# A two-layer sequence model on one core: skip term, tap order and y order changed, output product behind state product and flips

## The chip, the cores and the metric
The kernel runs on one core of a Trainium2 chip. The metric is the device time of one execution in microseconds, start to end, on that core. Lower is better. The engines are called PE (TensorE), DVE (VectorE), ACT (ScalarE), POOL (GpSimd) and SP (the queue that issues the transfers).

## What is computed
Two layers over 1024 tokens of width 512 (2 sequences of 512). Attention and a binary-weight product come first, and take the first 394 us. Then comes a state-space mixer, which is nearly all of the rest, and at the end an expert layer. The mixer, cut to what matters here:

```python
dA = dt * A; cum = cumsum(dA)                       # per head, inside a chunk
scores  = (C @ B.T) * exp(cum_i - cum_j) * dt       # causal
y_intra = scores @ x
states  = (dt * exp(cum_last - cum) * B).T @ x
s       = exp(cum_last) * s + states                # carried from chunk to chunk
y_inter = (C * exp(cum)) @ s_previous
y = y_intra + y_inter + D * x                       # D * x is the skip term
g = y * silu(gate)                                  # gate = a projection of the input
g = g * rsqrt(mean(g * g) + eps) * norm_w           # mean over a group of 1024 channels
out = g @ out_w.T                                   # x, B, C = silu(conv4(projection))
```

There are 128 heads of 64 channels in 8 groups, and the state has 128 entries.

## The kernel before
The mixer handles a group of 16 heads in two halves (units) of 8 heads (512 channels). A unit has 8 steps, one for each chunk of 128 tokens, and chunks 0 to 3 are the first sequence, 4 to 7 the second. So a group has 16 steps, numbered k = 0 to 15, with chunk c = k % 8, and there are 128 steps in all. Each engine has its own in-order program for a step, written by hand, and the engines meet through semaphores. There is no scheduler: what stands first on an engine runs first, and an instruction that waits holds back all behind it.

A step "carries" (`carries(c)`) when a state comes in from the chunk before: every c but 0 and 4. It "feeds" (`feeds(c)`) when it must leave a state: every c but 3 and 7. So c = 1, 2, 5, 6 do both.

PE in a step: the transposes and product for the scores (first unit only), the gate projection for a later phase (`project_gate`, 12 matmuls), the product with the carried state (`p_inter`, L1664), one or two convolution inputs for the next unit (`conv_event`, 12 matmuls each into `p_mix`), the output product of the step before (`project_out`, 12 matmuls into `p_out`), the state product (L1677), the flips of x to token order for the next step (`flip_x`, L1582), the intra product (L1688), and a sum of squares of the step before (L1599). In c = 0 and 4 a `first_flip` (L1582 too) also flips this step's own x, which must have left the convolution. `project_out` waits for `y_split`, the low part of y of the step before.

The way of y: the intra product lands in `p_intra`. DVE adds the skip term (`xskip`, L1968) and multiplies by silu(gate) (L1973). ACT copies the high part (`high_y`, L1737), DVE subtracts to get the low part (`y_low_part`, L1921), then PE may run `project_out`. In a carrying step `xskip` is D * x plus the carried part, made by four instructions of 128 columns (L1957). In c = 0 and 4 it is D * x alone, made ahead of the taps by four instructions from and to SBUF (L1960).

The way of a convolution: ACT makes the first tap (`first_tap`, L785), DVE adds three more (`taps_of`, L807), ACT applies silu (`channels_of`, L795). For an x tile that silu also waits for the skip term of this step (`xskip_done`), since it overwrites x:

```python
if e[0] == "x":
    act.wait_ge(xskip_done, step(g, k) + 1)
```

ACT also makes the decay exponentials (L1773, four and four around `high_y`), the token copy of x (`empty_x`, L1730), which POOL turns into the operands of the state and intra products, and silu of the gate (`silu_gate`, L1783). Exponential and silu each need their own table (ACT_TABLE_LOAD). DVE also makes the arguments of the exponentials (L1912), the state's decay and sum (L2018, L2043), and reads the sum of squares of two steps ago (`mean_square`, L1930) at the head of a step. The p_inter product of step s waits for that read (`ms_read`) and for the state.

## Time and profile before
| what | value |
|---|---|
| median of 3 runs | 2118.3 us (2116.76 to 2119.54) |
| the profiled execution: its own time | 2118.76 us |
| its span, first to last instruction | 2116.9 us |
| PE busy | 1983.2 us, 94% |
| DVE busy | 1709.6 us, 81% |
| ACT busy | 1440.5 us, 68% |
| POOL busy | 1260.6 us, 60% |
| mean granted TensorE clock | 0.98 of full |

The table is read with care: a share of busy time is a mean over stages. The mixer runs from about 394 us to 2047 us of the span, a group of 16 steps takes some 205 us in the middle, and all groups but the first and the last look alike. Times inside a stretch are counted from the start of the span.

### The profile page before, as it was taken

The numbers are of one execution on the slowest core, as the hardware profiler recorded it, in microseconds if no ns is written. First come the engines' busy times: TensorE is split into PE (matmuls) and PEld (weight loads), VectorE is DVE, ScalarE is ACT, GpSimd is POOL, SyncE is SP. The second block draws the span as 40 slices with busy tenths as digits, with TensorE's granted clock in tenths as the row PEclk, the third lists the DMA queues.
The fourth block names the chain that finished last, engine by engine and source line by source line (L and its number), as shares of the span: only waits on it lengthen the run. The fifth ranks groups of instructions, "written<-read, shape, count | busy, mean of one in ns | idle before, by whom it ended". The sixth has DMA issues, their size and how long they took to land.

```text
span 2116.9 us, 34073 instructions
## 1 busy us (share of the span) xinstructions
PE 1983.2 (94%) x11288; PEld 1531.2 (72%) x11288; DVE 1709.6 (81%) x3231; ACT 1440.5 (68%) x2755; POOL 1260.6 (60%) x1185
## 2 busy tenths in 40 slices
PE   8999987799999999999999999999999999999878
PEld 4666666587877787778777777777777777777655
DVE  5677765588898889888888888888888888988976
ACT  1466633577777777777777777777778777777721
POOL 4355330256766676767676767675767666756651
PEclk9899998899999999999999999999999999999989
DMA  4000010332223322332323232222222322222201
GB/s 169 1 0 0 0 56 1 99 108 92 95 72 102 110 71 83 101 115 70 103 72 115 65 109 91 99 86 89 95 91 80 94 99 96 81 90 80 94 21 40
DMA packets 125707, 166.04 MB, mean 78 GB/s; under 512 B 37777, under 2 KB 88977, under 8 KB 121330
## 3 DMA queue, kind: packets, MB, share of 16 engines
q1 hardware_dynamic: 125554, 164.11, 24.0%
q8 instruction: 83, 1.36, 0.3%
q14 instruction: 70, 0.57, 0.1%
HBM read 159.88 MB, written 4.20 MB: 78 GB/s over the span
## 4 chain that ended last, share of the span: by engine, by line
ACT 32%; PE 26%; DVE 20%; issue 7%; POOL 0%; SPq 0%; ACTq 0%; DMA 0%; POOLq 0%; DVEq 0%
DVE conv L807 12%; ACT wq_t L1773 7%; PE p_mix L102 7%; PE p_gate_intra L102 6%; ACT L1773 5%; ACT L1783 4%; PE p_out L102 4%; DVE x_skip L1960 3%; ACT conv L785 2%; ACT x_and_gate L1783 2%; ACT yT L1737 2%; PE p_gate_intra L1688 2%; ACT y_squares L1743 2%; PE pM L102 2%; ACT w_gate L1715 1%
## 5 line engine op out<-in xcount | busy, mean ns | idle before, releaser
L2124 POOL TENSOR_TENSOR wq_t<-wq_t,cb 128x1024 f32<-128x1024 f32 x128 | 314.4, 2457 | 197.4 <-ACT wq_t L1773 159.9
L102 PE MATMUL p_out<-w_out,yT 128*128 128x512 f32 x1536 | 382.8, 399 | 24.0 <-issue 14.7
L102 PEld LDWEIGHTS p_out<-w_out,yT 128*128 128x128 f32 x1536 | 290.3, 191 | 99.8 <-issue 20.8
L102 PE MATMUL p_gate_intra<-x_high,w_gate 128*128 128x512 f32 x1024 | 350.1, 403 | 5.9 <-POOL w_gate L2107 3.4
L102 PE MATMUL p_mix<-x_high,w_x 128*128 128x512 f32 x1024 | 351.8, 405 | 2.1 <-DVE x_low L1148 1.4
L807 DVE SCALAR_TENSOR_TENSOR conv<-p_mix,unit_small,conv 128x511 f32<-128x511 f32 (+2 forms) x384 | 286.9, 747 | 63.0 <-ACT conv L785 51.4
L1773 ACT ACTIVATE wq_t<-wq_t,minus_cum 128x128 f32<-128x128 f32 x1024 | 325.3, 390 | 1.4
L795 ACT ACTIVATE x_and_gate<-conv 128x512 f32<-128x512 f32 x128 | 80.8, 632 | 253.9 <-DVE conv L807 253.7
L2165 POOL TENSOR_TENSOR x_to_state<-x_tokens,group_dt_end 128x512 f32<-128x512 f32 x96 | 120.8, 1258 | 176.6 <-ACT x_tokens L1730 176.6
L102 PEld LDWEIGHTS p_gate_intra<-x_high,w_gate 128*128 128x128 f32 x1024 | 193.4, 189 | 44.5 <-POOL w_gate L2107 3.7
L102 PEld LDWEIGHTS p_mix<-x_high,w_x 128*128 128x128 f32 x1024 | 193.7, 189 | 41.5 <-DVE conv L807 1.9
L102 PE MATMUL p_mix<-x_low,w_x 128*128 128x512 f32 x512 | 201.0, 393 | 0.0
L102 PE MATMUL p_gate_intra<-x_low,w_gate 128*128 128x512 f32 x512 | 200.9, 392 | 0.0
L1912 DVE TENSOR_TENSOR wq_t<-cum_all,tables_in 128x1024 f32<-128x1024 f32 x128 | 196.6, 1536 | 4.0 <-DMA cum_all<-cum_rows 3.0
L2170 POOL TENSOR_TENSOR x_dt<-x_tokens,tables_in 128x512 f32<-128x512 f32 x128 | 169.2, 1322 | 42.1 <-ACT x_tokens L1730 38.0
L1921 DVE TENSOR_TENSOR yT<-p_gate_intra,yT 128x512 fp32r<-128x512 f32 x128 | 88.1, 688 | 86.1 <-ACT yT L1737 86.1
L1773 ACT ACT_TABLE_LOAD x118 | 151.4, 1283 | 2.1
L826 POOL TENSOR_TENSOR w_x<-w_raw_tiles,w_x 128x512 fp32r<-128x512 f32 x64 | 83.1, 1299 | 107.3 <-DVE w_x L815 107.3
L1783 ACT ACT_TABLE_LOAD x110 | 141.1, 1283 | 1.9
L1688 PE MATMUL p_gate_intra<-wq_t,x_dt 128*64 128x128 f32 x2048 | 140.1, 279 | 0.4 <-POOL wq_t L2124 0.4
L476 DVE CUSTOM_DVE_ANT_0 pF<-pF,row_mask 128x128 f32<-128x128 f32 (+3 forms) x256 | 115.9, 526 | 24.7 <-PE pF L293 24.7
L1688 PEld LDWEIGHTS p_gate_intra<-wq_t,x_dt 128*64 128x64 f32 x2048 | 109.2, 136 | 28.2 <-issue 26.4
(242 smaller groups left out, 4435.2 us busy)
## 6 DMA issues: line engine op xcount, KB each, us to landing
cum_all<-cum_rows SPq DMA_DIRECT2D x128, 512.0 KB, 3.8
exp_cum<-exp_rows SPq DMA_DIRECT2D x192, 128.0 KB, 3.2
w_staged<-in_w_gate SPq DMA_DIRECT2D x16, 1024.0 KB, 5.4
w_raw_tiles<-in_w_x SPq DMA_DIRECT2D x64, 256.0 KB, 3.1
w_staged<-in_w_out SPq DMA_DIRECT2D x16, 1024.0 KB, 4.9
w_raw_tiles<-in_w_bc SPq DMA_DIRECT2D x16, 256.0 KB, 5.3
x<-in_x SPq DMA_DIRECT2D x1, 2048.0 KB, 18.6
out<-x_and_gate SPq DMA_DIRECT2D x8, 256.0 KB, 2.0
```

Source lines behind the costliest of these rows:

```text
L102: last = pe.matmul(dst, left[a](k), right[b](k), start=k == 0 and n_ == 0, stop=stop and k == tiles - 1 and n_ == 2)
L476: m = dve.tensor_tensor_reduce(pF[:, b, n_ * wide:(n_ + 1) * wide], pF[:, b, n_ * wide:(n_ + 1) * wide], row_mask[:, CPS * P - wide:], 1.0 ...
L807: m = dve.scalar_tensor_tensor(self.conv[:, par, back:], self.p_mix[:, bank, 0:SEQ - back], w[:, TAPS - 1 - back:TAPS - back], self.conv[: ...
L826: pool.tensor_tensor(self.wx[:, 1, j], self.raw[:, j % 2], self.wx[:, 0, j].bitcast(F32), ALU.subtract).then_inc(self.x_w_split, 1)
L1688: m = pe.matmul(p_intra[a * HEAD_P:(a + 1) * HEAD_P, j * P:(j + 1) * P], xdt[:, h], decay[:, k % 2, h], start=True, stop=True)
L1773: m = act.activation(decay[:, k % 2, h], decay[:, k % 2, h], ACT.Exp, bias=neg[:, s // STEPS % 2, c, head:head + 1])
L1783: act.activation(tile_of(SG, phase, j), p_gate.rearrange("p (q t) -> p q t", t=P), ACT.Silu).then_inc(sg_done, 1)
L1912: dve.tensor_tensor(decay[:, k % 2], cumB[:], over(tab[:, s // STEPS % 2, 0, c, mine], P), ALU.min).then_inc(arg_done, 1)
L1921: dve.tensor_tensor(yT[:, 1].rearrange("p j t -> p (j t)"), p_intra, yT[:, 0].rearrange("p j t -> p (j t)").bitcast(F32), ALU.subtract).th ...
L2124: pool.tensor_tensor(decay[:, k % 2], decay[:, k % 2], cb[:, c].unsqueeze(1).to_broadcast([P, UNIT_HEADS, P]), ALU.mult).then_inc(decay_do ...
L2165: pool.tensor_tensor(xs[:], xtok[:], over(dtend[:, c, mine], HEAD_P), ALU.mult).then_inc(xs_done, 1)
L2170: pool.tensor_tensor(xdt[:], xtok[:], over(tab[:, g % 2, 1, c, mine], HEAD_P), ALU.mult).then_inc(xdt_done, 1)
```

## The change
Four edits, all inside the mixer.

1. PE: in steps with c = 1, 2, 5, 6 `project_out` stands behind the state product and `flip_x`, directly ahead of the intra product. In the others it stays.
2. Skip term in c = 0 and 4: no `xskip`. Once the intra product is there, four DVE instructions of 128 columns add D * x into `p_intra` in PSUM, and the separate sum is gone. The wait of `square_sums` follows.
3. ACT: the first tap of the first convolution stands ahead of `silu_gate` (and its table load). In c = 4 `high_y` stands ahead of the first four exponentials. In c = 0 all silu of convolutions stand behind `empty_x`; the very first step makes its gate silus together.
4. DVE: in c = 7 the taps stand ahead of `out_halves`, `make_y` and `y_low_part`.

```diff
@@ -1667,7 +1667,8 @@
                                 m.then_inc(inter_done, 1)
                             for i, e in convs:
                                 conv_event(i, e)
-                            project_out(*before)
+                            if c % CPS in (0, CPS - 1):
+                                project_out(*before)
 
                         if feeds(c):
                             pe.wait_ge(xs_done, n_feeds(g, k) + 1)
@@ -1679,6 +1680,8 @@
                         if (k + 1) % CPS:
 
                             flip_x(g, k + 1)
+                        if c % CPS in (1, CPS - 2):
+                            project_out(*before)
 
                         pe.wait_ge(decay_done, s + 1)
                         pe.wait_ge(xdt_done, s + 1)
@@ -1689,7 +1692,7 @@
                                           decay[:, k % 2, h], start=True, stop=True)
                         m.then_inc(intra_done, 1)
                         if before:
-                            wait(pe, xskip_done, s + 1)
+                            wait(pe, xskip_done, s + 1 if carries(c) else s)
                             square_sums(*before, p_inter)
 
                 groups(pe, group)
@@ -1823,31 +1826,30 @@
                             for i, e in convs:
                                 first_tap(i, *e)
                             if not before:
-                                silu_gate(-2)
-                            channels_of(convs[0][1][0], convs[0][1][2], PLAN.conv_parity(k, convs[0][1][0]), g, k)
-                            if not before:
+                                for tile in (-2, -1, 0):
+                                    silu_gate(tile)
                                 out_high_part(g * 2 + half, half)
                             if half:
                                 keep_half(*before)
-                            if before:
-                                empty_x(g, k + 1)
-                            for i, (e, _, index) in convs[1:]:
+                            empty_x(g, k + 1)
+                            for i, (e, _, index) in convs:
                                 channels_of(e, index, PLAN.conv_parity(k, e), g, k)
-                            if not before:
-                                silu_gate(-1)
-                                silu_gate(s)
-                                empty_x(g, k + 1)
                             continue
 
+                        if c == CPS:
+                            high_y(*before)
                         decay_exps(s, k, 0, UNIT_HEADS // 2)
-                        high_y(*before)
                         if c == CPS:
                             empty_x(g, k)
+                        else:
+                            high_y(*before)
                         decay_exps(s, k, UNIT_HEADS // 2)
                         square_y(*before)
+                        for i, e in convs[:1]:
+                            first_tap(i, *e)
                         if s + AHEAD < TILES:
                             silu_gate(s)
-                        for i, e in convs:
+                        for i, e in convs[1:]:
                             first_tap(i, *e)
                         if c == CHUNKS - 1:
                             if half and last:
@@ -1951,24 +1953,25 @@
 
                     half, c = divmod(k, CHUNKS)
                     src = chunk_of(X, c // CPS, c % CPS)
+                    dst, add = (xskip, p_inter) if carries(c) else (p_intra.rearrange("p (j t) -> p j t", t=P), p_intra)
                     for j in range(UT):
-                        gain = skip[:, g % 2, half, j:j + 1]
-                        if carries(c):
-                            m = dve.scalar_tensor_tensor(xskip[:, j], src[:, j], gain, p_inter[:, j * P:(j + 1) * P],
-                                                         ALU.mult, ALU.add)
-                        else:
-                            m = dve.tensor_scalar(xskip[:, j], src[:, j], gain, None, ALU.mult)
+                        m = dve.scalar_tensor_tensor(dst[:, j], src[:, j], skip[:, g % 2, half, j:j + 1],
+                                                     add[:, j * P:(j + 1) * P], ALU.mult, ALU.add)
                     m.then_inc(xskip_done, 1)
 
                 def make_y(g, k):
 
                     s, c = step(g, k), k % CHUNKS
                     dve.wait_ge(intra_done, s + 1)
-                    dve.wait_ge(xskip_done, s + 1)
-                    dve.tensor_tensor(p_intra[:], p_intra[:], xskip[:].rearrange("p j t -> p (j t)"),
-                                      ALU.add).then_inc(y_sum, 1)
+                    if carries(c):
+                        dve.wait_ge(xskip_done, s + 1)
+                        dve.tensor_tensor(p_intra[:], p_intra[:], xskip[:].rearrange("p j t -> p (j t)"),
+                                          ALU.add).then_inc(y_sum, 1)
+                        dve.wait_ge(y_sum, n_carries(g, k) + 1)
+                    else:
+                        skip_part(g, k)
+                        dve.wait_ge(xskip_done, s + 1)
                     dve.wait_ge(sg_done, (s // CPS + 1) * CPS)
-                    dve.wait_ge(y_sum, s + 1)
                     tiles = p_intra.rearrange("p (j t) -> p j t", t=P)
                     dve.tensor_tensor(tiles, tiles, chunk_of(SG, c // CPS, c % CPS), ALU.mult).then_inc(y_done, 1)
 
@@ -2017,12 +2020,8 @@
                                     dve.wait_ge(exps_done, g + 1)
                                 dve.tensor_tensor(state[:], state[:], over(exps[:, 1, c, mine], HEAD_P),
                                                   ALU.mult).then_inc(state_steps, 1)
-                        else:
-                            dve.wait_ge(conv_done, len(PLAN.first) if first and k == 0 else
-                                        PLAN.ready(g, k - 1, ("x", UT - 1, c // CPS)))
-                            if not s:
-                                dve.wait_ge(in_tables, 80)
-                            skip_part(g, k)
+                        elif not s:
+                            dve.wait_ge(in_tables, 80)
                         if last and half and c > 1:
                             out_sum(g, c - 2)
                         if half and c in (1, 2) and not last:
@@ -2046,12 +2045,12 @@
 
                         convs = [(i, e) for i, e in enumerate(events) if e[0][0] != "cb"]
                         if c == CHUNKS - 1:
+                            taps_of(convs)
                             if half and not last:
                                 out_halves(*before)
                             make_y(g, k)
                             if not (last and half):
                                 y_low_part(g, k)
-                            taps_of(convs)
                             if last and half:
                                 ahead_norm(k)
                             continue
```

PE in step 1 of the second group, from the end of the convolution input to the sum of squares. The names in brackets are the semaphores that an instruction waits for. Before:
```order
L102 MATMUL p_mix<-x_high,w_x 128x512
L102 MATMUL p_out<-w_out,yT 128x512 [waits out_free,y_split,out_split]
L102 MATMUL p_out<-w_out,yT 128x512 x11
L1677 MATMUL p_inter_state<-x_to_state,b_tokens 128x512 [waits state_done,cb_done,xs_done]
L1582 MATMUL p_flip<-ident,x_and_gate 128x128 [waits flip_emptied]
L1582 MATMUL p_flip<-ident,x_and_gate 128x128 x3
L1688 MATMUL p_gate_intra<-wq_t,x_dt 64x128 [waits sq_done,xdt_done,decay_done]
L1688 MATMUL p_gate_intra<-wq_t,x_dt 64x128 x7
L1599 MATMUL p_inter_state<-one_column,y_squares 128x1 [waits ms_read,squares_summed,xskip_done]
```
and of the change:
```order
L102 MATMUL p_mix<-x_high,w_x 128x512
L1678 MATMUL p_inter_state<-x_to_state,b_tokens 128x512 [waits state_done,cb_done,xs_done]
L1582 MATMUL p_flip<-ident,x_and_gate 128x128 [waits flip_emptied]
L1582 MATMUL p_flip<-ident,x_and_gate 128x128 x3
L102 MATMUL p_out<-w_out,yT 128x512 [waits out_free,y_split,out_split]
L102 MATMUL p_out<-w_out,yT 128x512 x11
L1691 MATMUL p_gate_intra<-wq_t,x_dt 64x128 [waits sq_done,xdt_done,decay_done]
L1691 MATMUL p_gate_intra<-wq_t,x_dt 64x128 x7
L1599 MATMUL p_inter_state<-one_column,y_squares 128x1 [waits ms_read,squares_summed,xskip_done]
```
The twelve matmuls of the output product went from ahead of the state product to between flips and intra product.

DVE in step 12 (c = 4, two convolutions), from the low part of y to the product with the gate. Before:
```order
L1921 TENSOR_TENSOR yT<-p_gate_intra,yT 128x512 [waits y_high]
L1960 TENSOR_SCALAR x_skip<-x_and_gate,skip_in 128x128 [waits conv_done]
L1960 TENSOR_SCALAR x_skip<-x_and_gate,skip_in 128x128 x3
L807 SCALAR_TENSOR_TENSOR conv<-p_mix,unit_small,conv 128x511 [waits tap_first]
L807 SCALAR_TENSOR_TENSOR conv<-p_mix,unit_small,conv 128x510 [waits taps_done]
L807 SCALAR_TENSOR_TENSOR conv<-p_mix,unit_small,conv 128x509 [waits taps_done]
L807 SCALAR_TENSOR_TENSOR conv<-p_mix,bc_small,conv 128x511 [waits tap_first]
L807 SCALAR_TENSOR_TENSOR conv<-p_mix,bc_small,conv 128x510 [waits taps_done]
L807 SCALAR_TENSOR_TENSOR conv<-p_mix,bc_small,conv 128x509 [waits taps_done]
L815 CAST w_x<-w_raw_tiles 128x512 [waits in_raw1]
L2045 COPY state<-p_inter_state 128x512 [waits st_done]
L1968 TENSOR_TENSOR p_gate_intra<-p_gate_intra,x_skip 128x512 [waits xskip_done,intra_done]
L1973 TENSOR_TENSOR p_gate_intra<-p_gate_intra,x_and_gate 128x512 [waits y_sum,sg_done]
```
and of the change:
```order
L1923 TENSOR_TENSOR yT<-p_gate_intra,yT 128x512 [waits y_high]
L807 SCALAR_TENSOR_TENSOR conv<-p_mix,unit_small,conv 128x511 [waits tap_first]
L807 SCALAR_TENSOR_TENSOR conv<-p_mix,unit_small,conv 128x510 [waits taps_done]
L807 SCALAR_TENSOR_TENSOR conv<-p_mix,unit_small,conv 128x509 [waits taps_done]
L807 SCALAR_TENSOR_TENSOR conv<-p_mix,bc_small,conv 128x511 [waits tap_first]
L807 SCALAR_TENSOR_TENSOR conv<-p_mix,bc_small,conv 128x510 [waits taps_done]
L807 SCALAR_TENSOR_TENSOR conv<-p_mix,bc_small,conv 128x509 [waits taps_done]
L815 CAST w_x<-w_raw_tiles 128x512 [waits in_raw1]
L2044 COPY state<-p_inter_state 128x512 [waits st_done]
L1958 SCALAR_TENSOR_TENSOR p_gate_intra<-x_and_gate,skip_in,p_gate_intra 128x128 [waits intra_done]
L1958 SCALAR_TENSOR_TENSOR p_gate_intra<-x_and_gate,skip_in,p_gate_intra 128x128 x3
L1976 TENSOR_TENSOR p_gate_intra<-p_gate_intra,x_and_gate 128x512 [waits sg_done,xskip_done]
```
The four L1960 in front of the taps and the sum L1968 are gone, and four instructions on `p_intra` (L1958 now) stand behind the wait for the intra product.

ACT in the same step, from the squares of y to the token copy. Before:
```order
L1743 ACTIVATE y_squares<-p_gate_intra 128x512 [waits ms_product,y_split]
L1783 ACT_TABLE_LOAD [waits y_done]
L1783 ACTIVATE x_and_gate<-p_gate_intra 128x4x128 [waits gate_done]
L785 ACTIVATE conv<-p_mix,unit_small 128x512 [waits conv_done,mix_done,in_small0]
L785 ACTIVATE conv<-p_mix,bc_small 128x512 [waits conv_done,mix_done]
L795 ACTIVATE x_and_gate<-conv 128x512 [waits taps_done,xskip_done]
L795 ACTIVATE bc_channels<-conv 128x512 [waits taps_done]
L1715 ACTIVATE w_gate<-w_staged 128x512 [waits gate_done]
L1754 ACTIVATE attn<-attn,inv_rms 128x512 [waits rms_done,out_free]
L1730 ACTIVATE x_tokens<-p_flip 128x512 [waits xdt_done,flip_done]
```
and of the change:
```order
L1746 ACTIVATE y_squares<-p_gate_intra 128x512 [waits ms_product,y_split]
L785 ACTIVATE conv<-p_mix,unit_small 128x512 [waits conv_done,mix_done,in_small0]
L1786 ACT_TABLE_LOAD [waits y_done]
L1786 ACTIVATE x_and_gate<-p_gate_intra 128x4x128 [waits gate_done]
L785 ACTIVATE conv<-p_mix,bc_small 128x512 [waits conv_done,mix_done]
L795 ACTIVATE x_and_gate<-conv 128x512 [waits taps_done,xskip_done]
L795 ACTIVATE bc_channels<-conv 128x512 [waits taps_done]
L1718 ACTIVATE w_gate<-w_staged 128x512 [waits gate_done]
L1757 ACTIVATE attn<-attn,inv_rms 128x512 [waits rms_done,out_free]
L1733 ACTIVATE x_tokens<-p_flip 128x512 [waits xdt_done,flip_done]
```
The first L785 moved past the table load and the gate silu. The silu L795 waits for `xskip_done` as before, but that is now given behind the intra product, and the token copy stands behind it.

## Rows read from the trace of the kernel before
**Rows 1.** The windows view, one stretch of 200 us in the middle of the mixer.
```profile
700.00:900.00 200.00, 193.65 (x1085) 153.56 (x1084) 171.42 (x281) 154.73 (x294) 135.80 (x111) 1.00 0.29 93
```
**Rows 2.** The waits view, TensorE, whole span: total us, times, longest.
```profile
PE p_flip L1582 <- ACT x_and_gate L795: 16.7, 15, 1.2
PE p_out L102 <- issue: 14.7, 15, 1.5
PE p_inter_state L1664 <- DVE mean_square L1930: 11.2, 6, 4.4
...
PE p_out L102 <- DVE yT L1921: 9.2, 19, 1.3
...
PE p_inter_state L1664 <- DVE sum_squares L1928: 5.0, 7, 0.7
```
**Rows 3.** The groups view, forms kept apart: the two skip operations of VectorE.
```profile
L1957 DVE SCALAR_TENSOR_TENSOR x_skip<-x_and_gate,skip_in,p_inter_state 128x128 f32<-128x128 f32 x384 | 107.8, 343 | 3.4
...
L1960 DVE TENSOR_SCALAR x_skip<-x_and_gate,skip_in 128x128 f32<-128x128 f32 x128 | 101.6, 854 | 8.3 <-ACT x_and_gate L795 8.3
```
**Rows 4.** The timeline, TensorE, steps 0 and 1 of a group (start, duration, [idle before]).
```profile
816.53 2.91 PE L102 MATMUL p_out<-w_out,yT 128*128 128x512 f32 x12
820.69 0.66 PE L1582 MATMUL p_flip<-ident,x_and_gate 128*128 128x128 f32 x4 [1.25 <-ACT x_and_gate L795]
...
828.09 1.09 PE L1688 MATMUL p_gate_intra<-wq_t,x_dt 128*64 128x128 f32 x16
...
837.88 3.01 PE L102 MATMUL p_out<-w_out,yT 128*128 128x512 f32 x12 [1.47 <-issue]
```
**Rows 5.** The timeline, ScalarE, step 15 into step 0.
```profile
809.24 1.28 ACT L1783 ACT_TABLE_LOAD   x1
...
811.03 0.77 ACT L785 ACTIVATE conv<-p_mix,unit_small 128x512 f32<-128x512 f32 x1
...
818.71 1.28 ACT L795 ACT_TABLE_LOAD   x1 [1.53 <-DVE conv L807]
820.01 0.63 ACT L795 ACTIVATE x_and_gate<-conv 128x512 f32<-128x512 f32 x1
```
**Rows 6.** The timeline, VectorE, the same stretch.
```profile
809.23 1.12 DVE L1957 SCALAR_TENSOR_TENSOR x_skip<-x_and_gate,skip_in,p_inter_state 128x128 f32<-128x128 f32 x4
...
813.27 0.70 DVE L1968 TENSOR_TENSOR p_gate_intra<-p_gate_intra,x_skip 128x512 f32<-128x512 f32 x1 [0.34 <-PE p_gate_intra L1688]
...
816.05 2.31 DVE L807 SCALAR_TENSOR_TENSOR conv<-p_mix,unit_small,conv 128x511 f32<-128x511 f32 x3
```
**Rows 7.** The timeline, VectorE, steps 3 and 4 of the same group.
```profile
865.25 2.31 DVE L807 SCALAR_TENSOR_TENSOR conv<-p_mix,unit_small,conv 128x511 f32<-128x511 f32 x3 [1.78 <-ACT conv L785]
...
873.02 5.07 DVE L1960 TENSOR_SCALAR x_skip<-x_and_gate,skip_in 128x128 f32<-128x128 f32 x4
```
**Rows 8.** The timeline, TensorE, step 5 of the same group.
```profile
882.87 1.13 PE L1664 MATMUL p_inter_state<-bc_channels,state 128*128 128x128 f32 x8 [0.70 <-DVE sum_squares L1928]
```
**Rows 9.** The timeline, TensorE, step 8 of the group before.
```profile
713.28 3.02 PE L102 MATMUL p_out<-w_out,yT 128*128 128x512 f32 x12 [0.54 <-DVE yT L1921]
717.50 0.66 PE L1582 MATMUL p_flip<-ident,x_and_gate 128*128 128x128 f32 x4 [1.20 <-ACT x_and_gate L795]
```
**Rows 10.** The timeline, ScalarE, end of step 12 of that group.
```profile
775.99 0.64 ACT L795 ACTIVATE bc_channels<-conv 128x512 f32<-128x512 f32 x1 [1.53 <-DVE conv L807]
...
777.66 0.58 ACT L1730 ACTIVATE x_tokens<-p_flip 128x512 f32<-128x512 f32 x1
```
**Rows 11.** The timeline, VectorE, steps 13 and 15 of that group.
```profile
781.35 0.69 DVE L1921 TENSOR_TENSOR yT<-p_gate_intra,yT 128x512 fp32r<-128x512 f32 x1 [0.34 <-ACT yT L1737]
...
805.45 0.15 DVE L1933 TENSOR_SCALAR mean_square<-mean_square 128x1 f32<-128x1 f32 x1
```
**Rows 12.** The timeline, TensorE, steps 12 and 15 of that group.
```profile
774.68 1.09 PE L1688 MATMUL p_gate_intra<-wq_t,x_dt 128*64 128x128 f32 x16
...
805.56 1.13 PE L1664 MATMUL p_inter_state<-bc_channels,state 128*128 128x128 f32 x8
```

## The prediction
> **What bounds the kernel now.** I read the windows view first. In 200 us in the middle of the mixer PE is busy for 193.65 at full clock, DVE for 171.42 [rows 1]. So PE sets the pace, and what this change can give there is PE's idle time alone. It adds and removes no matmul. The waits view then names that idle time [rows 2]: flips of step 0 or 8 wait for a silu of ACT (16.7 us, 15 times), output products wait in 15 places for something the view does not name (14.7) and in 19 for the low part of y (9.2), and the product with the carried state waits for a reading of squares (11.2 and 5.0). The sum is 56.8 us, the bound of what can be won in these waits. But PE is not alone. A second loop runs through DVE and ACT in each carrying step: low part of y, skip, state decay, taps, silu, token copy, exponentials, high part of y. The timeline shows it nearly without slack in steps 13 to 15: DVE idles only 0.34 us before the low part of y [rows 11], and PE's product with the carried state follows DVE's reading of squares within 0.1 us (DVE's last reading begins at 805.45, PE at 805.56) [rows 11, 12]. So a delay given to that loop there comes out at PE.
>
> **What the skip edit saves and costs.** The four L1960 cost 854 ns each, 101.6 us in all; L1957, the same shape with one operand in PSUM, costs 343 [rows 3]. No row shows a skip instruction that reads and writes PSUM. Bounds: four L1957 span 1.12 us [rows 6], four at their full 343 are 1.37, and below, one whole-width sum such as L1968 is 0.70 [rows 6]. I take 1.12, the same shape and instruction. In 32 steps DVE so loses 4 x 0.854 = 3.4 us ahead of the taps and has 1.12 in place of 0.70 behind the intra product: y comes 0.4 us later behind it. The first is a gain only where DVE is late there. It is in step 4, where the four took 5.07 us [rows 7].
>
> **Steps 15, 0 to 3 (seven groups).** The flip of step 0 starts at 820.69 after 1.25 us of idling [rows 4], behind a silu at 820.01 whose table load came at 818.71 after 1.53 us of waiting for taps [rows 5]; the taps ran 816.05 to 818.36, behind y [rows 6]. Now ACT's first tap goes ahead of the table load at 809.24 [rows 5] and is done at 809.3 + 0.8 = 810.1, and DVE's taps follow the skip that ends at 810.35 [rows 6], until 812.7. The sum of half outputs (0.69) brings DVE to 813.4, against 813.27 before [rows 6], so y is not later. ACT no longer waits: load and silu start 1.5 us earlier, the flip is ready when the output product ends at 816.53 + 2.91 = 819.4 [rows 4]. Gain 1.25.
>
> In step 1 the output product waits 1.47 us (837.88) [rows 4]. It waits for y_low: intra ends at 828.09 + 1.05 = 829.14, and 8.74 us later PE may start. Now state product and flips (from the same rows of the order, about 1.4 us on PE) go first, and y is 0.4 later. All but some 0.3 is covered: gain 1.1. DVE however only moves up by about 1 us in all, PE by 2.4. In step 2 the carried-state product therefore waits for the reading of squares, which I put at 0.6. Net of steps 0 to 3: 1.25 + 1.1 - 0.6 = 1.75. Times 7: **12.3 us**.
>
> **Steps 4 to 7 (seven groups).** In step 3 the taps waited 1.78 us for ACT's first tap [rows 7], which now comes 1.8 us sooner; in step 4 the 5.07 us are gone, and high y is ahead of the exponentials. DVE runs so 2.8 us ahead of before. That ends the wait of 0.70 at 882.87 [rows 8] and a wait for y in step 4. The latter I put at 0.23: the 9.2 [rows 2] less 8 x 0.54 for step 8 [rows 9] leaves 4.9, a third of it for step 4 and the rest for the last group. I add 0.45, an estimate, for the tails of matmuls that an unhindered next one would overlap (the twelve of an output product take 2.91, tail included [rows 4]), as three instructions wait here. Sum 1.4. Times 7: **9.8 us**.
>
> **Steps 8 to 11 (eight groups).** At step 8 the output product waits 0.54 for y and the flip 1.20 [rows 9]. ACT's eight exponentials stand ahead of high y there, so the 0.54 stays; the flip's 1.20 goes, as in step 0, for the taps are ahead of y. Step 9 has an output wait of 0.55 (the 14.7 less 7 x 1.47, over 8) [rows 2, 4], which state product and flips cover. Two waits for the squares of 0.1 to 0.3 come in its place. Net 1.2 + 0.6 - 0.3 = 1.5. Times 8: **12.0 us**.
>
> **Steps 12 to 15: where the change costs (seven groups).** Here two convolutions fill DVE and ACT. Intra of step 12 ends at 774.68 + 1.05 = 775.73 [rows 12]. ACT's x silu had long been made, at 775.99 came the silu of B or C, and the token copy began at 777.66, 1.67 later [rows 10]. Now the x silu waits for the skip term, which is there at 775.74 + 1.2 = 776.95. Then x silu, 0.53 later the other one, and 1.67 later the copy: 776.95 + 0.53 + 1.67 = 779.15. That is 1.5 us later than 777.66. Behind the copy on ACT stand the table load, the exponentials and high y, so DVE's low y of 781.35 [rows 11] comes at 782.85. DVE had 0.34 of slack there and is full from then on (decay of state, six taps, sum, y, reading of squares). The reading for step 15's product comes 1.45 late, at 806.9 in place of 805.45 [rows 11]. PE waits for it: **-1.45 each, -10.2 us** for 7 groups. Bounds: if a shorter overlap with POOL gives DVE this time back, 0; if both step 14 and step 15 pay in full, -2.9 each.
>
> **The ends.** The last group has no convolutions from step 12. What is left of the 9.2 when step 8 (8 x 0.54) and step 4 (7 x 0.23) are taken off is 3.3 in its last steps [rows 2, 9]; state product and flips cover most. I take 2. The waits of up to 4.4 there for the squares [rows 2] stay, since layer norms of DVE stand ahead of the reading. The gate silus of the first step change little: 0, within 1.
>
> **The sum.** 12.3 + 9.8 + 12.0 - 10.2 + 2.0 = 25.9 us. Against the profiled execution's 2118.76 (span 2116.9, so 1.9 lie around it) that is 2092.9; the median of the runs is 2118.3, 0.5 lower. I predict **2093 us**, 1.2% less.
>
> **The rivals.** (a) *Full gain*: DVE's relief removes the loss of steps 12 to 15 and the new waits for squares. Then 12.3 + 9.8 + 12.0 + 2 plus 7 x 0.6 and 8 x 0.3 = 43, 2076 us. For it: DVE loses 80 us of work in all (101.6 [rows 3] + 32 x 0.70 - 128 x 0.343). Against: the removed work sits in front of an idle stretch in step 12, not in steps 13 to 15. (b) *The second loop decides*: PE's gains are given back within the unit, as the DVE and ACT loop, not PE, sets every carrying step; only what shortens that loop stays. Then the flips' 16.7 stay, step 4's relief stays at half (5), steps 12 to 15 cost 10.2: 12 us, 2106. For it: the 0.1 us between reading and product [rows 11, 12]. (c) *Slower*: the x silu behind the skip term delays the token copy in steps 0, 4, 8 and 12 alike. If all four lost 1.5 at PE, 30 x 1.5 = 45 against gains of 36: 2128. It decides once more than three of four such delays reach PE. Against: in step 4 the old skip had made the copy just as late, and in steps 0 and 8 the copy now goes first. (d) *Nothing happens*: the waits are named by releasers that are only the last of several, and others of the same lateness stand behind them. Then within 4 us of 2118.
>
> The Trainium skill (VectorE: DVE Perf Modes, The TRN2 errata) charges each instruction with PSUM input a fixed 120 cycles, by which four of 128 columns would be about 1.03 us. By it y would come 0.1 us earlier than by the 1.12 of the rows, which changes nothing.
>
> **Chances.** Main case 0.5, (a) 0.12, (b) 0.2, (c) 0.1, (d) 0.08. No change means within 0.2% (4.2 us), about what a measurement of this kernel can tell. Faster takes the main case, (a) and (b): 0.82. Slower gets 0.1, same 0.08. The range takes in (a) and (b): 2073 to 2112; the likeliest case alone spans 2083 to 2103 (its loss from 0 to -2.9 in seven groups).
>
> **What would show it.** In the profile after: flips waiting for ACT near 0 in place of 16.7; no unnamed wait of the output product in steps 1 and 9; a product with the carried state that waits 1.5 to 2 us in step 15 and some 0.5 in steps 2 and 9; L1958 in PSUM near 343 ns; ACT's token copy of step 13 some 1.5 us later behind the intra product. I am wrong if the waits for the squares or the state grow by more than 25 us in all, if the tap goes later because the convolution is not yet there when ACT asks, or if the intra product starts to wait for the exponentials.

## The result and the profile after

The changed kernel takes 2091.25 us (median of 4 runs, 2086.8 to 2094.25) against 2118.71 us for the kernel before (2116.76 to 2119.54): ratio 0.987, 95% interval 0.985 to 0.989. The profiled execution took 2094.25 us with a span of 2092.5, so 24.4 us less span than before. The forecast was 2093.

The windows view of the changed kernel, the same stretch as [rows 1]; the columns are again time, then busy time and instructions of PE, PEld, DVE, ACT and POOL, clock, DMA share and GB/s:
```profile
700.00:900.00 200.00, 196.70 (x1104) 155.11 (x1104) 164.88 (x279) 156.69 (x296) 138.66 (x113) 1.00 0.29 94
```
PE gained 3.05 us of work in 200 us and now idles for 3.3. DVE is busy for 6.5 us less. The waits view, TensorE, answers to [rows 2]:
```profile
PE p_inter_state L1664 <- DVE mean_square L1932: 17.7, 24, 4.4
...
PE p_out L102 <- DVE yT L1923: 7.2, 9, 0.8
PE p_inter_state L1599 <- issue: 6.1, 15, 0.6
...
PE p_inter_state L1664 <- DVE sum_squares L1930: 3.2, 8, 0.4
```
The waits of the flips (16.7) are gone, and the unnamed waits of the output product are down from 14.7 us to 1.3, in 7 places. The reading of squares is waited for longer (17.7 in place of 11.2, 24 times in place of 6), and the sum of squares L1599 has a wait of its own (6.1 us, 0.6 in one place before). The groups view shows the skip in its two forms:
```profile
L1958 DVE SCALAR_TENSOR_TENSOR x_skip<-x_and_gate,skip_in,p_inter_state 128x128 f32<-128x128 f32 x384 | 107.8, 343 | 3.4
...
L1958 DVE SCALAR_TENSOR_TENSOR p_gate_intra<-x_and_gate,skip_in,p_gate_intra 128x128 f32<-128x128 f32 x128 | 36.1, 349 | 14.3 <-PE p_gate_intra L1691 14.2
```
The timeline, TensorE, steps 0 and 1 of the group of [rows 4] (start, duration, [idle before]):
```profile
816.29 2.93 PE L102 MATMUL p_out<-w_out,yT 128*128 128x512 f32 x12
819.18 0.66 PE L1582 MATMUL p_flip<-ident,x_and_gate 128*128 128x128 f32 x4
...
836.67 2.99 PE L102 MATMUL p_out<-w_out,yT 128*128 128x512 f32 x12 [0.17 <-issue]
841.28 0.35 PE L1599 MATMUL p_inter_state<-one_column,y_squares 128*128 128x1 f32 x2 [0.59 <-issue]
```
The flip follows the output product at once. The output product of step 1 waits 0.17 where it waited 1.47, and 0.59 of that comes back at L1599, the last product of step 1 (the table below counts it in step 2, since it stands behind the intra product). The view names no releaser for it, but the semaphore that it waits for is given by GpSimd, which adds up the squares. The timeline, GpSimd:
```profile
840.72 0.46 POOL L2152 TENSOR_TENSOR y_squares<-y_squares 128x128 f32<-128x128 f32 x1
```
It ends at 841.18, and TensorE goes on at 841.28.

All groups but the first and the last repeat, in most columns to some hundredths of a us and in the worst to 0.35, so the trace compares the time of four steps better than the medians do. The table is worked out from the start of the last matmul of the intra product in steps 15, 3, 7, 11 and 15 of each traced kernel, as a mean over the second to the seventh group, in us:

| kernel | median | steps 0-3 | 4-7 | 8-11 | 12-15 | group |
|---|---|---|---|---|---|---|
| before | 2118.7 | 53.07 | 48.69 | 51.98 | 51.65 | 205.39 |
| changed | 2091.25 | 51.47 | 47.13 | 50.74 | 52.89 | 202.24 |
| a, output product back | 2104.75 | 52.11 | 47.39 | 50.73 | 52.93 | 203.16 |
| c, both tap orders back | 2148.86 | 52.60 | 49.86 | 52.38 | 54.60 | 209.43 |
| c1, ScalarE's tap back | 2137.04 | 52.79 | 49.87 | 50.94 | 54.61 | 208.21 |
| c2, VectorE's taps back | 2114.17 | 52.74 | 47.14 | 52.27 | 52.89 | 205.04 |
| d, copy first | 2088.70 | 51.47 | 47.17 | 50.75 | 52.41 | 201.80 |
| e, squares ahead of y | 2091.18 | 51.80 | 47.16 | 50.16 | 52.45 | 201.57 |
| b, skip back | 2071.39 | 51.04 | 47.15 | 49.92 | 51.35 | 199.46 |
| b and e | 2071.84 | 51.04 | 47.17 | 49.71 | 51.35 | 199.27 |
| m, b with a wait | 2083.56 | 51.04 | 47.15 | 50.37 | 52.53 | 201.08 |
| r, b, first order back | 2072.55 | 51.04 | 47.16 | 50.14 | 51.35 | 199.68 |
| y, b, y order back | 2070.65 | 51.04 | 47.17 | 49.92 | 51.35 | 199.47 |
| i, output product alone | 2115.86 | 52.61 | 49.14 | 51.52 | 52.09 | 205.37 |

### The profile page after: what moved, and what is told of

Its sections match the earlier page's. It is cut to its first block, busy times and chain, and to the rows that moved or that the text cites. A ratio compares the mean times of both kernels' runs of the same rounds, so it can differ in the third digit from the quotient of the medians.

```text
span 2092.5 us, 34009 instructions
## 1 busy us (share of the span) xinstructions
PE 1982.6 (95%) x11288; PEld 1526.2 (73%) x11288; DVE 1631.6 (78%) x3199; ACT 1443.7 (69%) x2755; POOL 1262.6 (60%) x1185
## 4 chain that ended last, share of the span: by engine, by line
PE 57%; DVE 15%; ACT 9%; issue 4%; POOL 1%; SPq 0%; DMA 0%; POOLq 0%; ACTq 0%; DVEq 0%
PE p_mix L102 16%; PE p_out L102 13%; PE p_gate_intra L102 11%; PE p_gate_intra L1691 4%; DVE conv L807 4%; PE p_inter_state L1664 3%; PE p_inter_state L1678 3%; PE p_flip L1582 2%; ACT L1776 2%; ACT wq_t L1776 2%; DVE state L2021 2%; PE pM L102 2%; DVE x_skip L1958 1%; DVE p_gate_intra L1958 1%; PE p_inter_state L1599 1%
## 5 line engine op out<-in xcount | busy, mean ns | idle before, releaser
L102 PEld LDWEIGHTS p_out<-w_out,yT 128*128 128x128 f32 x1536 | 285.1, 190 | 73.2 <-DVE yT L1923 12.0
L795 ACT ACTIVATE x_and_gate<-conv 128x512 f32<-128x512 f32 x128 | 80.8, 632 | 259.6 <-DVE conv L807 156.5
L2164 POOL TENSOR_TENSOR x_to_state<-x_tokens,group_dt_end 128x512 f32<-128x512 f32 x96 | 112.6, 1173 | 125.0 <-ACT x_tokens L1733 125.0
L2169 POOL TENSOR_TENSOR x_dt<-x_tokens,tables_in 128x512 f32<-128x512 f32 x128 | 162.3, 1268 | 39.7 <-ACT x_tokens L1733 39.7
L1664 PEld LDWEIGHTS p_inter_state<-bc_channels,state 128*128 128x128 f32 x768 | 100.0, 195 | 38.0 <-issue 33.0
```

The source lines that it names most:

```text
L102: last = pe.matmul(dst, left[a](k), right[b](k), start=k == 0 and n_ == 0, stop=stop and k == tiles - 1 and n_ == 2)
L1664: m = pe.matmul(p_inter[:, j * P:(j + 1) * P], state[:, 2 * j:2 * j + 2].rearrange("p h e -> p (h e)"), BC[:, 1, cols], start=True, stop=True)
L2164: pool.tensor_tensor(xs[:], xtok[:], over(dtend[:, c, mine], HEAD_P), ALU.mult).then_inc(xs_done, 1)
L2169: pool.tensor_tensor(xdt[:], xtok[:], over(tab[:, g % 2, 1, c, mine], HEAD_P), ALU.mult).then_inc(xdt_done, 1)
```

## The experiments

The ratios below are against the kernel before on the same chip (2117.7 to 2118.7 us). The profiled execution of the changed kernel lay 3 us above its median, so differences of spans to it read some 3 us less loss, or 3 us more gain, than those of the medians; differences of medians are given where nothing else is said. The changed kernel was timed four times only (2086.8 to 2094.25), so such a difference is good to some 3 us; the column of the group is finer.

**a. The output product back at its old place.**
```diff
-                            if c % CPS in (0, CPS - 1):
-                                project_out(*before)
+                            project_out(*before)
...
-                        if c % CPS in (1, CPS - 2):
-                            project_out(*before)
```

> The changed kernel with the output product ahead of the state product and the flips again in every step (in steps 1, 2, 5, 6, 9, 10, 13 and 14 that is the old place); skip, taps and y order as changed. Theory (the moved product is what takes away the waits for yT in steps 1 and 9): TensorE waits for yT in front of the product again, about 1.1 us in step 1 and 0.5 to 1.0 us in step 9, so +1.6 to 2.1 us for each of 8 groups less some 0.7 that the wait for the squares in step 2 gives back: 2091 + 8 x 1.2 = about 2101 us, 2096 to 2106. Rival (the place is neutral: the squares behind the step wait for the same y, so that the stall only moves within the step): 2091 us within 3.

2104.75 us, ratio 0.9936 [0.9922, 0.9949]: 13.5 us slower than the changed kernel, and 10.6 by the spans (2103.1 against 2092.5), as the theory said (2096 to 2106). The timeline, TensorE, step 1:
```profile
838.90 3.00 PE L102 MATMUL p_out<-w_out,yT 128*128 128x512 f32 x12 [1.48 <-issue]
```
The old wait of step 1 is back, step by step 1.3 us, less 0.65 given back in step 2. Step 9 does not change: beside the other edits the state product and the flips cover nothing there. The last group loses 3.7 us, the others 0.9 each.

**i. The output product moved alone, on the kernel before.** The same lines with the sign turned.

> The kernel before with one part of the change alone: the output product behind the state product and the flip in steps 1, 2, 5, 6, 9, 10, 13 and 14. Theory (the move is worth as much here as in the changed kernel, where undoing it cost 13.5 us: it covers the wait for yT in step 1): 2118.5 - 13.5 = 2105 us, 2101 to 2110. Rival 1 (y is later in the kernel before, so that the wait only shortens, or moves to the squares behind the step): 2113 us or more. Rival 2 (the flips that now come sooner wait longer for ScalarE's silu, or gain as well): 2098 us or less.

2115.86 us, ratio 0.9982 [0.9972, 0.9993]. Rival 1 holds. Timeline, TensorE, steps 1 to 5:
```profile
839.13 2.99 PE L102 MATMUL p_out<-w_out,yT 128*128 128x512 f32 x12 [0.18 <-issue]
843.73 0.35 PE L1599 MATMUL p_inter_state<-one_column,y_squares 128*128 128x1 f32 x2 [0.59 <-issue]
...
874.40 3.03 PE L102 MATMUL p_out<-w_out,yT 128*128 128x512 f32 x12 [0.46 <-DVE yT L1924]
884.11 1.13 PE L1664 MATMUL p_inter_state<-bc_channels,state 128*128 128x128 f32 x8 [0.71 <-DVE sum_squares L1931]
```
The wait of step 1 goes in the same way (1.3 us), but the squares behind it take 0.7 of that and steps 3 and 4 another 0.57. Step 9 gains 0.8, and steps 10 and 13 lose 0.3 and 0.4. A middle group gains nothing (205.37 against 205.39); what is won comes from the last group. The same move is worth 13.5 us beside the other three edits (10.6 by the spans) and 2.7 alone. Which of the three makes the difference was not tried.

**c, c1, c2. The tap orders back, together and one by one.** c1 is the first piece, c2 the second, c both:
```diff
-                        for i, e in convs[:1]:
-                            first_tap(i, *e)
                         if s + AHEAD < TILES:
                             silu_gate(s)
-                        for i, e in convs[1:]:
+                        for i, e in convs:
                             first_tap(i, *e)
...
-                            taps_of(convs)
                             if half and not last:
                                 out_halves(*before)
                             make_y(g, k)
                             if not (last and half):
                                 y_low_part(g, k)
+                            taps_of(convs)
```

> The changed kernel with the orders around the taps undone outside the first step of a half: ScalarE's first tap behind the gate's silu again, and VectorE's taps of step 7 and 15 behind y again. Theory (the late taps of steps 7 and 15 are what made the flip of the next step wait for the silu of x): the wait of the flips comes back, 1.25 us in 7 groups and 1.2 us in 8, +18 us: 2107 us within 5. Rival (the new order of ScalarE in steps 0 and 8, token copy ahead of all silus, took the flip's wait away, and the taps hardly matter): 2091 to 2095 us, without a wait of the flips.

> The changed kernel with ScalarE's first tap behind the gate's silu again; VectorE's taps of steps 7 and 15 stay ahead of y. It splits the 58 us that undoing both cost. Theory (the stalls that came back in steps 4 to 6 and 13 and 14 are due to ScalarE's tap, those in steps 0 and 8, with the flips' wait, to VectorE's): 4.5 us a group, 2091 + 8 x 4.5 = 2127 us, 2118 to 2136, no wait of the flips. Rival (the two edits work on one loop, so that each alone costs most of the 58 us): over 2136 us. Rival 2 (VectorE's edit is nearly all): under 2105 us.

> The changed kernel with VectorE's taps of steps 7 and 15 behind y again; ScalarE's first tap stays ahead of the gate's silu. Theory (only steps 0 and 8 see it: 0.9 and 1.5 us a group, and the flips of these steps wait for the silu of x, some 1.2 us each): 2091 + 8 x 2.4 = 2110 us, 2102 to 2118. Rival (the taps are hidden once ScalarE's order is right): 2091 us within 4, no wait of the flips. Rival 2 (one loop with ScalarE's edit): over 2125 us.

c takes 2148.86 us (1.0147 [1.0132, 1.0163]), c1 2137.04 (1.0095 [1.0075, 1.0115]), c2 2114.17 (0.9982 [0.9967, 0.9996]). So the two orders carry 58 us, more than three times what I expected of them, and the larger part, 46 us, is ScalarE's first tap. c is even 31 us slower than the kernel before: the other edits without the tap orders are a loss. c2 came as its theory said, c1 lies just above its theory's range (2118 to 2136), where its rival begins. In c2 only steps 0 and 8 lose (1.3 and 1.4 us; step 9 adds 0.1), and the flips wait as before. The timeline of c2, TensorE and ScalarE, step 0:
```profile
824.01 0.66 PE L1582 MATMUL p_flip<-ident,x_and_gate 128*128 128x128 f32 x4 [1.47 <-ACT x_and_gate L795]
```
```profile
822.03 1.28 ACT L795 ACT_TABLE_LOAD   x1 [1.52 <-DVE conv L807]
```
These are [rows 4] and [rows 5] again: taps late, table load late, silu late, flip late. In c1 the flips do not wait; there the losses stand in steps 4 to 6 (2.7 us a group), 13 and 14 (1.7) and 0 (1.15). The timelines, VectorE in step 12 of c1, then of the changed kernel, and TensorE in steps 13 and 14 of c1:
```profile
984.64 2.32 DVE L807 SCALAR_TENSOR_TENSOR conv<-p_mix,unit_small,conv 128x511 f32<-128x511 f32 x3 [5.02 <-ACT conv L785]
```
```profile
969.84 2.32 DVE L807 SCALAR_TENSOR_TENSOR conv<-p_mix,unit_small,conv 128x511 f32<-128x511 f32 x3 [3.43 <-ACT conv L785]
```
```profile
992.15 1.13 PE L1664 MATMUL p_inter_state<-bc_channels,state 128*128 128x128 f32 x8 [0.58 <-DVE mean_square L1930]
1008.37 1.13 PE L1664 MATMUL p_inter_state<-bc_channels,state 128*128 128x128 f32 x8 [1.33 <-DVE mean_square L1930]
```
VectorE waits 5.0 us, 3.4 in the changed kernel, for a tap that stands behind a table load (1.28) and the gate's silu, and what follows on it, the reading of the squares for steps 13 and 14 included, comes later. Alone the two cost 46 + 23 = 69 us, together 58: step 0 loses 1.14 in c1, 1.27 in c2 and 0.96 in c, so its loss is counted twice in the 69.

**d. The token copy of steps 4 and 12 ahead of the silus.**
```diff
+                        if c == CPS:
+                            empty_x(g, k + 1)
                         for i, (e, _, index) in convs:
                             channels_of(e, index, PLAN.conv_parity(k, e), g, k)
...
-                        if (k + 1) % CPS:
+                        if (k + 1) % CPS and c != CPS:
                             empty_x(g, k + 1)
```

> The changed kernel with one instruction moved: in steps 4 and 12 ScalarE's copy of the next step's tokens stands ahead of the silus of x, not behind them. Theory (the loss of 0.7 us in step 14 and 0.5 us in step 15 comes from this copy, which stands behind a silu that waits for the skip, now behind the intra product): the stalls of steps 14 and 15 go, 7 x 1.24 = 9 us: 2082 us, 2079 to 2087. Rival 1 (the stalls of step 14 and 15 come from VectorE's reading of the squares alone): they stay, 2091 us within 3. Rival 2 (the silus of x, now behind the copy, make the flips of step 5 and 13 or the taps late): slower than 2094 us.

2088.70 us (0.9863 [0.9848, 0.9878]), 2.5 us faster: outside the theory's range (2079 to 2087) and inside that of rival 1 (2091 within 3). The trace agrees with neither in full: step 14 gives back 0.47 of its 0.69, step 15 nothing. The copy is only one of the things behind the silu of x: the exponentials and the high part of y still come after it.

**b. The skip of steps 0, 4, 8 and 12 back ahead of the intra product.** Edit 2 of the change reversed, all orders kept.

> The changed kernel with the skip term of steps 0, 4, 8 and 12 ahead of the intra product again, in its own tile and added by the wide addition of every step; all orders as changed. Theory (the skip behind the intra product frees VectorE at the head of the step, which gave 1.5 us in steps 4 and 5, and delays the silu of x and the token copy behind it, which cost 1.24 us in steps 14 and 15): the gain of steps 4 and 5 is lost, 8 x 1.5 = +12 us, the loss of steps 14 and 15 comes back, 7 x 1.24 = -9 us: 2094 us, 2088 to 2102, with the stalls of steps 14 and 15 gone in the trace. Rival 1 (the skip is behind most of the gain, in steps 0 and 8 too): another 8 x 1.3 lost on top, 2105 us or more. Rival 2 (the skip does nothing, the loss of steps 14 and 15 has another cause): the same stalls, 2091 us within 3.

2071.39 us (0.9779 [0.9766, 0.9793]): 20 us faster than the changed kernel. Theory and both rivals are wrong on the sum. The loss of steps 14 and 15 went as expected (1.54 us). Steps 4 to 7 did not change (47.15 against 47.13), so beside the other edits the skip edit had given them nothing, and steps 1, 9 and 10 gained 1.25 us more. Page, the chain that ended last, of the changed kernel and of b:
```profile
PE 57%; DVE 15%; ACT 9%; issue 4%; POOL 1%; SPq 0%; DMA 0%; POOLq 0%; ACTq 0%; DVEq 0%
```
```profile
PE 78%; ACT 3%; DVE 3%; issue 2%; POOL 1%; SPq 0%; DMA 0%; POOLq 0%; ACTq 0%; DVEq 0%
```
With the skip back VectorE and ScalarE have 6% of the chain between them, in place of 24%, and PE has 78%.

What changed in step 12 stands in the timelines. The changed kernel, TensorE, ScalarE and VectorE:
```profile
975.40 1.09 PE L1691 MATMUL p_gate_intra<-wq_t,x_dt 128*64 128x128 f32 x16
```
```profile
977.70 0.63 ACT L795 ACTIVATE x_and_gate<-conv 128x512 f32<-128x512 f32 x1 [5.32 <-DVE p_gate_intra L1958]
...
979.90 0.57 ACT L1733 ACTIVATE x_tokens<-p_flip 128x512 f32<-128x512 f32 x1
```
```profile
976.54 1.13 DVE L1958 SCALAR_TENSOR_TENSOR p_gate_intra<-x_and_gate,skip_in,p_gate_intra 128x128 f32<-128x128 f32 x4 [0.67 <-PE p_gate_intra L1691]
977.71 0.70 DVE L1976 TENSOR_TENSOR p_gate_intra<-p_gate_intra,x_and_gate 128x512 f32<-128x512 f32 x1
...
983.58 0.69 DVE L1923 TENSOR_TENSOR yT<-p_gate_intra,yT 128x512 fp32r<-128x512 f32 x1 [3.14 <-ACT yT L1740]
```
and of b:
```profile
968.45 1.09 PE L1691 MATMUL p_gate_intra<-wq_t,x_dt 128*64 128x128 f32 x16
```
```profile
969.49 0.58 ACT L1733 ACTIVATE x_tokens<-p_flip 128x512 f32<-128x512 f32 x1
```
```profile
970.33 0.70 DVE L1975 TENSOR_TENSOR p_gate_intra<-p_gate_intra,x_and_gate 128x512 f32<-128x512 f32 x1
...
973.17 0.69 DVE L1923 TENSOR_TENSOR yT<-p_gate_intra,yT 128x512 fp32r<-128x512 f32 x1
```
Counted from the start of the intra product, the gate product is 0.43 us later in the changed kernel (2.31 against 1.88), but the token copy is 3.46 later (4.50 against 1.04), and the low part of y 3.46 later too (8.18 against 4.72), behind 3.14 us in which VectorE stands still. ScalarE idled 5.32 us in front of a silu whose taps had long been made.

**m. b with the silus of x made to wait, nothing else.**
```diff
                     if e[0] == "x":
                         act.wait_ge(xskip_done, step(g, k) + 1)
+                        if not carries(k % CHUNKS):
+                            act.wait_ge(y_sum, step(g, k) + 1)
```

> The kernel with the skip of steps 0, 4, 8 and 12 ahead of the intra product (2071 us) and one added wait: in these steps ScalarE's silus of x also wait until VectorE has added the skip to the intra product, about 1.0 us behind the product's end. In the changed kernel they waited until 1.45 us behind it; y here is as early as in the run without this wait. Theory (the 20 us that the skip behind the intra product costs are mostly ScalarE's: the silu of x in step 12 stands 3 us later, and with it all that follows it in ScalarE's order): the loss of steps 14 and 15 comes back for the most part, 7 x 1.0, and some of that in steps 1, 9 and 10, 8 x 0.5: 2071 + 11 = 2082 us, 2077 to 2090. Rival (y is late by the skip that stands between the intra product and the gate product, and the silus are hidden): 2071 us within 3.

2083.56 us (0.9831 [0.9817, 0.9844]), as the theory said (2077 to 2090). The timeline, ScalarE, step 12 (its intra product starts at 972.51):
```profile
974.44 0.63 ACT L795 ACTIVATE x_and_gate<-conv 128x512 f32<-128x512 f32 x1 [4.94 <-DVE p_gate_intra L1972]
```
This wait alone brings back 12.2 of the 20 us: 1.18 of 1.54 in steps 12 to 15, 0.45 of 0.82 in steps 8 to 11, all in step 10. The silu starts here 1.93 us behind the start of the intra product, in the changed kernel 2.30, so the share of the wait there is rather larger. The 0.43 of step 1 and the gain of step 9 stay. By elimination those belong to the later y and to what stands behind it on VectorE; no run shows it directly.

**e, and b with e. The reading of squares ahead of the gate product.** `mean_square` of the step before stands in `make_y`, ahead of the wait for `sg_done`, and goes from its three old places.

> The changed kernel with VectorE's reading of the squares (of the step before) ahead of the gate product that makes y, in every step, in place of its two places behind y (the head of the next step but one, and behind y in steps 0 and 8). Theory (the skip behind the intra product makes y some 0.5 us later in steps 0, 4, 8 and 12, and what this costs TensorE is the wait for this reading: 0.66 us in step 2, 0.56 in 9, 0.31 in 10, 0.57 in 14, 0.82 in 15): most of 2.9 us a group goes, 2091 - 8 x 2.5 = 2071 us, 2066 to 2080. Rival (y itself is what is late, the reading only stands beside it; and the reading must now wait for the squares' product behind the intra product): 2088 us or more, with waits for yT in place of those for the reading.

> The changed kernel with the skip of steps 0, 4, 8 and 12 ahead of the intra product again (which gave 2071 us) and the reading of the squares ahead of the gate product that makes y. Theory (two edits against one stall: undoing the skip took away most waits for the reading, what is left is 0.66 us in step 2 and 0.12 us in step 9): 2071 - 8 x 0.7 = 2066 us, 2061 to 2071, and no more than 5 us under the run with the reading alone moved. Rival (they are separate): the sum of both gains, 2055 us or less. Rival 2 (the reading ahead of y holds y back where nothing waited for it): over 2073 us.

2091.18 us (0.9881 [0.9862, 0.99]) and 2071.84 (0.9793 [0.9771, 0.9814]): no gain in either median. The first is as its rival said; the second lies between its theory (2061 to 2071) and its rival 2 (over 2073). By the table a middle group gains 0.67 and 0.2 us, where the theory of e wanted 2.5. On the changed kernel the reading was indeed what steps 9 and 14 waited for (0.6 us each come back), but step 0 loses 0.33, step 15 loses 0.15, and the last group 1.3; the 0.66 of step 2 never was this reading. On b it takes 0.2 from step 9 and costs 3.9 in the last group. The rival's number is right. That y itself is late, its reason, can hold for no more than a part, since steps 9 and 14 did gain.

**r and y. The other two orders, on b.** r puts back ScalarE's order in steps 0 and 8 (the first piece of edit 3 in the diff of the change), y its order in steps 4 and 12. The edit of y:
```diff
-                        if c == CPS:
-                            high_y(*before)
                         decay_exps(s, k, 0, UNIT_HEADS // 2)
+                        high_y(*before)
                         if c == CPS:
                             empty_x(g, k)
-                        else:
-                            high_y(*before)
```

> The kernel with the skip ahead of the intra product (2071 us), with ScalarE's old order in steps 0 and 8: the silu of the first convolution ahead of the token copy for the next step (and of the gate's silus in the very first step). Theory (the wait of the flips in these steps was taken away by VectorE's early taps in steps 7 and 15, so the order here matters little): 2071 to 2077 us, no wait of the flips. Rival (the copy's place is a part of it: the flip of the next step and the intra product behind it wait for the copy): a silu of 0.63 us and its table load of 1.28 us ahead of the copy, up to 1.9 us in 15 steps, 2085 us or more.

> The kernel with the skip ahead of the intra product (2071 us), with ScalarE's old order in steps 4 and 12: high part of y behind the first half of the exponentials and ahead of the token copy. Theory (this order is what gave 0.4 us in step 4, while the 1.1 us of step 5 come from ScalarE's first tap): + 8 x 0.4, 2074 us, 2071 to 2078. Rival (it gave both): + 8 x 1.5, 2083 us, 2080 to 2087.

2072.55 us (0.9778 [0.9765, 0.9791]) and 2070.65 (0.977 [0.9757, 0.9783]). Both are within 1.2 us of b. The first costs 0.22 us in step 10 of each of seven groups and 1.15 in the last group, 2.3 by the spans; the second, for which the theory had 0.4 a group, costs nothing. So neither the skip nor the y order gave steps 4 to 7 anything; what they hang on is ScalarE's first tap (2.7 us in c1), and 0.26 on the output product (a). b, the fastest but for this last 0.7 us that the runs do not tell apart, stays the version to use.

The skip edit by itself on the kernel before was not tried: with ScalarE's old order in steps 0 and 8 the silu of x would stand ahead of the token copy and wait for a skip term that comes only behind the intra product.

## Why the prediction was right on the time, and on which steps

The sum for a middle group was 3.2 us and is 3.15 (205.39 less 202.24). That it comes so near is partly luck: the four terms below miss by 0.15 to 0.26 each, two down and two up. The last group gained 7.27 us (201.86 to 194.59; the sum has 1.75 + 1.4 + 1.5 + 2 = 6.65), the first lost 1.33 (185.52 to 186.85; the sum has +0.05), since its steps 1 and 2 have the new waits and no old ones to lose; "the gate silus of the first step change little" left that out. (Its first intra product stands 1.5 us later too, but between kernels that are alike up to there it stands anywhere from 421.2 to 425.1.)

- *Steps 0 to 3*: predicted 1.75, measured 1.60. The flip's wait and its cause, the late taps, are shown by c2 (1.27; step 0 itself gained 1.02 of the 1.25), the output product's 1.1 by a (1.3), the 0.6 given back in step 2 by both a and i (0.65 and 0.73). I put it down to the reading of squares, and that step is wrong. It is the sum of squares L1599, which waits 0.59 for GpSimd's adding up, and moving the reading (e) left it as it was.
- *The size of the skip*: four in PSUM take 1.13 us, I took 1.12.
- *Steps 4 to 7*: 1.4 against 1.56, right with one false source. I added ScalarE's earlier tap (1.8) and the 5.07 us of old skip. Without the tap these steps are slower than before (49.87 in c1); the skip gave nothing (b). The old skip sat in a stretch in which VectorE had time.
- *Steps 8 to 11*: 1.5 against 1.24. The flip's 1.2 is right (1.4 in c2), and step 8 gained 1.14, though "the 0.54 stays" is wrong: the waits view has the wait for y at up to 0.8. Step 9 gained 0.54 of 0.6, but not by the reason given: with the output product back at its old place it is as fast (a). Step 10 lost 0.42, where I took 0.3 for steps 9 and 10 together. The skip edit alone costs 0.82 here (b).
- *Steps 12 to 15*: -1.45 against -1.24. The copy came where I said: 4.50 us after the intra product's start against 2.98 before (777.66 less 774.68 [rows 10, 12]), 1.5 later. PE paid in steps 14 and 15 (0.69 and 0.53), not in 15 alone; the product with the carried state waits 0.4 in each, where I looked for 1.5 to 2 in step 15.

**What it missed.** It summed each place against the kernel before, and so never asked what each edit was worth beside the others. Beside the others the tap orders are worth 58 us and the skip edit costs 20. Rival (c), the silu of x behind the skip term, was half right: it is dear, in steps 8 to 15, and in the sum the gains of the other edits hid that. Rival (a) gave the full gain at 2076 and asked for VectorE's relief to remove the loss; b came to 2071 by leaving that relief out. Most of the 80 us of that relief came from what stood beside the old instructions and not from them: in b they cost 37.4 us in place of 101.6, as the last section shows.

## What to carry to other kernels

Price an edit also against the version that has all the others: here one of four took back 20 us while the whole was faster. Where an in-order engine has to wait for a value, look at everything that stands behind the waiting instruction; here the 3.5 us by which a silu held back copy, exponentials and high y cost at least 12.2 of the 20 us, more than the 0.4 us of later y. And put the first instruction of a chain that passes two engines (here a tap in front of a table load, 46 us) ahead of what is needed later.

## What was not expected of the hardware

The 854 ns of L1960 [rows 3] do not belong to the instruction. In b the same four instructions, in the same place in VectorE's program, take 352 ns in the mean; with the y order back 714. Groups view of b and of y:
```profile
L1962 DVE TENSOR_SCALAR x_skip<-x_and_gate,skip_in 128x128 f32<-128x128 f32 x128 | 37.4, 352 | 8.4 <-ACT x_and_gate L795 8.4
```
```profile
L1959 DVE TENSOR_SCALAR x_skip<-x_and_gate,skip_in 128x128 f32<-128x128 f32 x128 | 83.8, 714 | 8.4 <-ACT x_and_gate L795 8.4
```
The timeline, VectorE and GpSimd, step 4, first b, then y:
```profile
862.91 0.90 DVE L1962 TENSOR_SCALAR x_skip<-x_and_gate,skip_in 128x128 f32<-128x128 f32 x4
```
```profile
863.63 1.09 POOL L2167 TENSOR_TENSOR x_to_state<-x_tokens,group_dt_end 128x512 f32<-128x512 f32 x1 [0.49 <-ACT x_tokens L1733]
```
```profile
863.62 5.12 DVE L1959 TENSOR_SCALAR x_skip<-x_and_gate,skip_in 128x128 f32<-128x128 f32 x4
```
```profile
863.54 1.04 POOL L2164 TENSOR_TENSOR x_to_state<-x_tokens,group_dt_end 128x512 f32<-128x512 f32 x1 [0.27 <-ACT x_tokens L1733]
864.54 1.04 POOL L2169 TENSOR_TENSOR x_dt<-x_tokens,tables_in 128x512 f32<-128x512 f32 x1
865.54 2.43 POOL L2123 TENSOR_TENSOR wq_t<-wq_t,cb 128x1024 f32<-128x1024 f32 x1
867.94 0.72 POOL L2150 TENSOR_TENSOR y_squares<-y_squares 128x256 f32<-128x256 f32 x1
```
In b they start 0.7 us ahead of GpSimd's work and take 0.90 us together; in y they start 0.08 us behind its first instruction and take 5.12. Taken one by one in y's trace they end at 864.67, 865.67, 868.06 and 868.74, each within 0.1 us behind the end of one of the four GpSimd instructions shown (864.58, 865.58, 867.97, 868.66). So each of them lasts as long as the GpSimd instruction beside it, and the longest, 2.47 us, stands beside the one of 2.43. The Trainium skill (SBUF — State Buffer, Who interferes with whom) says that VectorE and GpSimd share a port pair as an exclusive lock, and that the order of issue, not the shape of the operation, decides who is blocked. The trace agrees: the same shape took 0.90 us ahead of GpSimd's instruction and 5.12 behind it. Those 4.2 us of VectorE make no difference to the time (2070.65 against 2071.39), so VectorE is not what step 4 waits for; in b it idles 2.13 us for ScalarE's tap behind the same four.
